# First experts: the first weights arrive as 2 KB pieces of two neighbouring rows, and the token transposes read every second column to match

## The reference, cut to what matters

```
# x2: (1250, 512) after attention and layernorm; E = 64 experts, TOP_K = 2, F = 256, H = 512
C = 2 * (T * TOP_K // E)                      # 78 places per expert
buf = zeros((E, C, H)).at[ef, posc].add(tok)  # each expert's tokens
h = gelu(einsum('ech,ehf->ecf', buf, w1) + b1[:, None, :])   # w1: (64, 512, 256)
y = einsum('ecf,efh->ech', h, w2) + b2[:, None, :]           # w2: (64, 256, 512)
ys = y[ef, posc] * (gf * keep)[:, None]       # each token adds its two gated rows
```

## Time and profile before

| | us |
|---|---|
| median of three runs | 1645.67 |
| profiled execution | 1641.68 |
| its span, from first to last instruction | 1640.0 |
| PE busy over the span | 1400.9 (85%) |
| DVE / ACT / POOL busy | 765.6 / 486.5 / 268.1 |
| first experts, first to last L1117 | 926.8 to 1189.2 |

### The profile page before, as it was taken

One profiled execution on the slowest core, in us unless ns is written; L12 is line 12 of the kernel. 1 busy time (PEld: TensorE's weight loads), 2 busy tenths in 40 slices (PEclk: granted clock), 3 DMA queues, 4 the chain that ended last, 5 costly groups with the idle time before them and its releaser, 6 DMA issues. The chain is left out here.

```text
span 1640.0 us, 23835 instructions
## 1 busy us (share of the span) xinstructions
PE 1400.9 (85%) x7657; PEld 919.8 (56%) x7658; DVE 765.6 (47%) x1503; ACT 486.5 (30%) x1191; POOL 268.1 (16%) x355
## 2 busy tenths in 40 slices
PE   0578888998997999999977699999989999649969
PEld 0347776444545666666645566666634555646642
DVE  5639999557215666666645332222232011533421
ACT  0137777001105555555502111111151001211111
POOL 5004444000000000000011122222250000002224
PEclk9999999999999999999987699999999999658997
DMA  5000000002000000000042399999950000623336
GB/s 138 0 1 1 0 0 0 26 0 77 0 4 23 1 1 1 1 1 1 1 144 63 110 331 330 331 323 327 303 135 3 0 0 0 234 61 102 128 97 168
DMA packets 93976, 142.34 MB, mean 87 GB/s; under 512 B 13205, under 2 KB 50475, under 8 KB 93783
## 3 DMA queue, kind: packets, MB, share of 16 engines
q1 hardware_dynamic: 69655, 98.12, 19.5%
q0 software_dynamic: 14976, 26.81, 5.9%
q10 hardware_dynamic: 9280, 16.52, 2.9%
HBM read 115.09 MB, written 26.29 MB: 86 GB/s over the span
## 5 line engine op out<-in xcount | busy, mean ns | idle before, releaser
L1117 PEld LDWEIGHTS ps<-b_r 128*128 128x128 f32 x1024 | 127.9, 196 | 34.4 <-issue 32.8
L869 DVE TENSOR_REDUCE b_row_max<-ps 125x1 f32<-125x1251 f32 x80 | 116.5, 1456 | 60.3 <-PE ps L770 60.3
L1117 PE MATMUL ps<-b_r 128*128 128x78 f32 x1024 | 125.8, 277 | 1.1 <-DVE b_r L1178 1.1
L1126 PE MATMUL ps<-b_r 128*78 128x512 f32 x256 | 122.0, 600 | 0.0
L445 ACT ACTIVATE b_r<-b_r 125x125 f32<-125x125 f32 x330 | 107.7, 389 | 45.8 <-DVE b_r L400 45.7
L473 PE MATMUL ps<-b_r 125*125 125x160 f32 x660 | 119.4, 317 | 0.0
L428 POOL TENSOR_TENSOR b_r<-b_r 125x160 f32 x110 | 82.4, 749 | 163.7 <-ACT b_r L439 162.4
L1021 POOL TENSOR_TENSOR b_x<-b_x,b_r 125x512 f32<-125x512 f32 x10 | 12.7, 1268 | 582.0 <-DVE b_r L967 582.0
L802 PE MATMUL ps<-b_r 125*64 125x125 f32 x1600 | 94.7, 272 | 10.1 <-ACT b_r L833 9.4
L1162 ACT ACTIVATE b_r<-ps,b_r 128x78 f32<-128x78 f32 x128 | 34.7, 323 | 228.9 <-PE ps L1117 228.9
L770 PE MATMUL ps<-b_r 64*125 64x417 f32 (+1 forms) x480 | 96.9, 536 | 6.0 <-ACT b_r L841 4.7
(11 more groups left out here) (252 smaller groups left out, 2237.1 us busy)
## 6 DMA issues: line engine op xcount, KB each, us to landing
b_r<-L_ffn_w SPq DMA_DIRECT2D x128, 512.0 KB, 10.3
y<-b_r ACTq DMA_DIRECT2D x64, 156.0 KB
b_r<-L_ffn_W SPq DMA_DIRECT2D x2, 4096.0 KB, 20.0
y<-b_r ACTq DMA_DIRECT2D x24, 256.0 KB, 2.4
rows<-b_r SPq DMA_DIRECT2D x2, 2400.0 KB
b_x<-x SPq DMA_DIRECT2D x1, 2400.0 KB
out<-b_x SPq DMA_DIRECT2D x10, 240.0 KB
y<-b_r SPq DMA_DIRECT2D x1, 2048.0 KB, 11.1
```

The source lines that it names most:

```text
L869: link(dve.tensor_reduce(T.row_max[:, slot:slot + 1], T.ps[:P, 3 * h:3 * h + 3, 0:CW], AX.XY, ALU.max))
L1117: last = pe.matmul(T.ps[:, 2 + r % 2, f * CAP:(f + 1) * CAP], T.ew1[r % WS][:, k, f * 128:(f + 1) * 128], T.ex_t[:, r % 2, k, :], start=(k ...
L1126: last = pe.matmul(T.ps[:CAP, 4 + r % 2, :], T.eh[:, r % 2, f, :], T.ew2[r % WS][:, f, :], start=(f == 0), stop=(f == FK - 1))
```

## The change

`load_expert` describes the load of `w1` in another way. Rows `h * 256 + 2 * p` and `h * 256 + 2 * p + 1` (h is 0 or 1) now go to partition `p` as one piece of 2 KB. A partition gets two pieces instead of four, and the same 2 KB of each half stand next to each other in DRAM and in SBUF. The load of 512 KB is made of 256 pieces instead of 512. The DMA of `w2`, the number of DMAs, their order and the slots are as before.

On partition `p` the four steps of the sum are now features `2p`, `2p + 1`, `256 + 2p` and `256 + 2p + 1`. The transposes at L1107 take their 128 columns from `first` on with a step of two: `first` is 0, 1, 256 and 257. All else, the number and order of instructions on every engine too, is as it was.

```
 def load_expert(sp, T, S, A, e, slot):
 
-    sp.dma_start(T.ew1[slot], A.L0_ffn_w1[bass.ds(e, 1)].rearrange("o (k p) f -> p (o k) f", k=KD))\
+    sp.dma_start(T.ew1[slot].rearrange("p (h k) f -> p h (k f)", k=2),
+                 A.L0_ffn_w1[bass.ds(e, 1)].rearrange("o (h p k) f -> p (o h) (k f)", h=2, k=2))\
       .then_inc(S.ew_loaded[slot], 16)
...
                 for k in range(KD):
-                    last = pe.transpose(T.ps[:, r % 2, k * CAP:(k + 1) * CAP], T.ex[:CAP, r % 2, k * 128:(k + 1) * 128],
+                    first = k // 2 * 256 + k % 2
+                    last = pe.transpose(T.ps[:, r % 2, k * CAP:(k + 1) * CAP], T.ex[:CAP, r % 2, first:first + 255:2],
                                         T.ident[:CAP, :CAP])
```

## The result

The change makes the kernel slower, by less than half a per cent: 1646.69 us against 1638.82 us, medians of 20 runs each, ratio 1.0045 with a 95% interval of 1.0024 to 1.0067. That is 4 to 11 us. The forecast was 1642 us in a range of 1626 to 1660, within 1%, with a small gain inside it. The time lies inside the range and the sign was wrong. That it lies inside is no support for the sum: the range was wide for the spread of the runs and for rival C, and neither of them made the kernel slower.

What follows compares the result with a forecast made beforehand. Gather latency, raised by DMA traffic, was taken to bound the first experts' steps. Terms -3.7 + 1.4 + 0 gave about -2 us, 1640 us against the profiled execution, put at 1642 us; range 1626 to 1660 us.

Steps and rivals of the forecast that it cites:

- rival C: First experts: the gather waits behind a number of weight pieces, not bytes; +49 us, 1690 us, chance 0.14.
- 20 us is all that the stage can give: First experts: 56 steps at 4.10 us against TensorE's own 3.74 leave a surplus of 20 us.
- the loop's 4.10: First experts: transposes to next gather's issue 1.45 us, landing 6.8 us, together two steps: 4.12 us each, 4.10 measured.
- the transposes with a step of two: L1107 in the first experts: reading every second float32 column costs 0, at the other end +5.7 us.
- the -3.7 us of the pieces: Weight loads in the first experts: fewer, larger pieces save 0.12 us in 31 of 56 steps.
- The price of a step: DMA time that 2 KB pieces save per step in the first experts: 0.12 us, between 0 and 0.25.
- So the queue must drain first: First experts: the weight queue, about 3 us over its shortest landing, takes 25 of 56 steps to empty before any gain.
- this sign: First experts: if `w1` lands earlier and the gather doesn't follow, the full queue was not what delays it.
- the rule's zero: By line rate from 512 bytes, 1 KB and 2 KB pieces move alike, so the pieces gain 0.
- The gather beside larger pieces: First experts: gathers land after 6.85 us instead of 6.8, +1.4 us, with ends of -3 and +6 us.
- Rival B: First experts: gather latency falls below 6.0 us, steps take 3.74 us; -20 us, 1621 to 1625 us, chance 0.12.
- Rival D: Load of `w1`: pieces still cut at 1 KB, only the transposes' 0 to +6 us left; counted within no measurable change.

Runs made afterwards that it cites:

- light: The kernel before, with SP's loop (experts 8 to 63) loading only a quarter of `w1`: ratio 0.9885 to the kernel before, 19 us faster.
- deep: The kernel before with four token slots instead of two and each gather issued one expert earlier: ratio 0.9984 to the kernel before, 2.6 us faster.
- step_only: The kernel before with the change's transposes (every second column) and the old 1 KB load of `w1`: ratio 1.0040 to the kernel before.
- pieces_only: The kernel before with the change's 2 KB load of `w1` and the old dense transposes: ratio 1.0005 to the kernel before.

## Why the prediction was right or wrong, point by point

**The bound was read rightly.** That the steps are held up by the gather's latency, that this comes from the DMA traffic, and that 20 us is all that the stage can give: light took 19 us off and ran at 3.75 us a step, and deep removed the gather's waits and ran at 3.72 us in its first half. What the text didn't see is how close the next bound stood: the transport with 1 KB pieces sustains 4.20 to 4.29 us a step, against the loop's 4.10, and only the weights loaded ahead keep it off the path.

**The step that failed first is "the transposes with a step of two", taken as 0.** It measures 217 ns for 141, 0.21 us in a turn, which is just the other end that the text had named ("0.2 us per turn", +5.7 us). The row that I took as the nearest, L467 in bf16, reads every second element of two bytes, so its columns stand 4 bytes apart like those of a dense float32 read. It was near in elements and not in bytes. Whether the distance in bytes or the type makes the difference no run shows, since none has a bf16 load with a wider step. In the loop the 0.21 us enter once in two steps: (6.7 + 1.66) / 2 = 4.18 us, measured 4.16. Over 56 steps half of 0.21 us is 5.9 us, and the paces measured, 4.16 and 4.10, give 3.4. Against that stand 4.6 us in the profiled stages, 6.6 for the step alone and 7.4 for the whole, the latter two with intervals from 3 to 10 and from 4 to 11 us. step_only's longer steps come from a gather at 6.9 us instead of 6.7 beside the old pieces; why it came later there is open.

The rule in the Trainium skill, "Advanced Engine Details and Errata", SBUF Cachelines, that two hits in a line keep full speed, does not hold for this read. A step of two (two hits in a line) and a step of four (one hit) both cost 217 ns.

**The second is the -3.7 us of the pieces.** The price of a step was set at 0.12 us, between 0 and 0.25. Where the transport binds the runs show 0.2 to 0.3, at the upper end, and with 0.25 the forecast would have been -11 us and further off. What held is that a full queue hides it. What failed was "So the queue must drain first", and that it would within 25 steps. The loads of `w1` from 960 to 1000 us in the changed kernel:

```profile
DMA to landing us min/median/max: 6.7/7.1/7.4
```

They land in 7.1 us there and in 7.4 from 1100 to 1160. The queue stopped growing and never emptied, and the gather stayed at 6.7. The gain exists only in the kernels in which the gather's loop is gone. The prediction had set this sign itself: the loads land earlier, SP is free again, and the gather doesn't follow, so the length of the queue is not what delays it. Why the gather still needs 6.7 us beside a shorter queue is not settled.

That answers the other rule of the Trainium skill as well ("DMA: Bandwidth & Descriptors", Specifications, line rate from 512 bytes on). In the kernels with four slots all the traffic moved at 329 GB/s with `w1` in 1 KB pieces and at 341 to 344 with 2 KB pieces; with 4 KB pieces 351 were moved at TensorE's own pace. So by these runs pieces of 1 KB do not move as fast as those of 2 KB, and the rule does not hold for this traffic. In the change itself the rule's zero was right, for another reason.

**The gather beside larger pieces** was forecast at 6.85 us from two gathers and measured 6.7, the text's own low end (-3 us). With it rival C fell, as pieces_only showed by itself. Rival B did not come: it needed a latency below 6.0 us, and even without the loop the 2 KB pieces sustained 3.99 us a step and not 3.74. Rival D fell with the packet counts.

Added up, the step at its measured price (+5.9), the pieces at nothing and the gather at 6.7 us (-2.8) give +3 us by the forecast's own sum. That is near the 3.4 of the paces and the 4.6 of the stages, and a little below the interval of the times, 4 to 11 us.

## What to carry to other kernels

A cost that is set to nothing because a nearby row shows none needs a row that is near in every respect. Here it was near in elements, and differed in type and in bytes between columns. Where a loop waits for the latency of one small transfer, making the large transfers cheaper gives nothing until that transfer is issued earlier; after that it does, so the order of the two changes matters. A mean over a stage can hide two stretches, as in deep, where weights loaded ahead covered the first half. And a wait that shrinks is a gain only if the work around it did not grow by as much.

## What the runs showed of the hardware that I had not expected

- A float32 weight load of 128 columns in TensorE took 141 ns dense and 217 ns with a step of two or of four columns.
- With `w1` in 1, 2 and 4 KB pieces, beside the same other traffic and with four token slots, all DMA traffic together moved at 329, 341 and at least 351 GB/s.
- A VectorE pass over 125 x 512 float32 went from 752 to 1106 ns when its operands were read and written regrouped.
- A gather of 78 rows landed in 4.2 us when a step moved 0.98 MB, and in 6.7 or 6.8 when it moved 1.37 MB, with the loads of `w1` landing in 7.4 us (the change) or in 10.5 (before).
